# One strip of a fused convolution loads all its window rows instead of taking its middle row by direct matmuls

## What is computed

```python
# 1: mix the 4x4 patches of 8x8 pixels and the channels, and add the input
out = einsum('oi,nikj->nokj', g_weight, patches(x)) + x          # -> cen
# 2: for each shift 1 and 3 and four directions: product of the two differences
prod = (cen - shifted(cen, d)) * (cen - shifted(cen, -d))
att  = max over shifts of (min over directions) + mean over shifts of (min over directions)
# 3: depthwise 3x3 convolution, 1x1 convolution, gate
g = pointwise(depthwise3x3(att))
result = cen * sigmoid(g) + cen
```

## Time and profile before

| | us |
|---|---|
| Median of 3 runs | 104.37 |
| Lowest and highest run | 103.74, 104.5 |
| The profiled execution | 103.87 |
| Its span, first to last instruction | 102.1 |
| Busy TensorE / VectorE / ScalarE / GpSimd | 83.3 / 89.9 / 54.4 / 86.7 |

### The profile page before, as it was taken

One profiled execution on the slowest core, in us unless ns is written; L12 is line 12 of the kernel. 1 busy time (PEld: TensorE's weight loads), 2 busy tenths in 40 slices (PEclk: granted clock), 3 DMA queues, 4 the chain that ended last, 5 costly groups with the idle time before them and its releaser, 6 DMA issues.

```text
span 102.1 us, 2342 instructions
## 1 busy us (share of the span) xinstructions
PE 83.3 (82%) x924; PEld 43.2 (42%) x924; DVE 89.9 (88%) x129; ACT 54.4 (53%) x94; POOL 86.7 (85%) x79
## 2 busy tenths in 40 slices
PE   4997899999999659494998759997355988969970
PEld 2196788777787322222322212324021224413430
DVE  6044699999999999999999999999799999999970
ACT  3201455555576573945756995198674314708620
POOL 6400999999999999999999999999999999877600
PEclk9999999999999999999999999999999999999999
DMA  3999500000000079920039930203988535960085
GB/s 45 353 290 394 185 6 0 6 0 6 0 3 6 0 137 172 250 99 0 0 65 234 260 100 6 103 0 75 232 268 278 117 70 116 231 129 6 0 316 198
DMA packets 7306, 12.14 MB, mean 119 GB/s; under 512 B 800, under 2 KB 2816, under 8 KB 7296
## 3 DMA queue, kind: packets, MB, share of 16 engines
q1 hardware_dynamic: 6768, 10.93, 39.1%
q10 hardware_dynamic: 528, 1.07, 3.4%
HBM read 3.22 MB, written 2.10 MB: 52 GB/s over the span
## 4 chain that ended last, share of the span: by engine, by line
DVE 51%; PE 20%; POOL 11%; issue 6%; ACT 5%; DMA 4%; POOLq 0%; DVEq 0%; ACTq 0%
DVE slots L705 19%; DVE m L723 17%; PE slots L927 8%; POOL u L235 8%; DVE m L702 6%; PE slots L893 5%; DMA early<-in_first_dram 4%; PE acc L868 3%; ACT slots L599 2%; POOL m L527 2%; PE acc L812 2%; PE slots L812 2%; DVE u L235 1%; POOL early L399 1%; ACT early L625 1%
## 5 line engine op out<-in xcount | busy, mean ns | idle before, releaser
L235 POOL TENSOR_TENSOR u<-cen 128x1056 f32<-128x1056 f32 (+9 forms) x38 | 65.0, 1771 | 6.4 <-DVE u L235 6.4
L599 ACT ACTIVATE slots<-u 128x1024 f32<-128x1024 f32 (+2 forms) x43 | 32.0, 762 | 25.8 <-POOL u L235 16.9
L705 DVE TENSOR_TENSOR slots<-slots,u 128x1024 f32<-128x1024 f32 (+2 forms) x33 | 29.6, 895 | 0.9 <-ACT slots L599 0.9
L723 DVE TENSOR_TENSOR m<-slots,m 128x1024 f32<-128x1024 f32 (+1 forms) x27 | 25.7, 952 | 0.9
L822 PE MATMUL acc<-early 128*32 128x256 f32 (+1 forms) x512 | 24.8, 353 | 0.9 <-DVE cen L693 0.6
L822 PEld LDWEIGHTS acc<-early 128*32 128x32 f32 x512 | 19.9, 110 | 5.6 <-DVE cen L693 0.9
L927 PE MATMUL acc<-early,wc 128*32 128x512 f32 x120 | 13.7, 595 | 5.0 <-DMA early<-att 3.8
L868 PE MATMUL acc<-cen,eye 128*128 128x512 f32 (+1 forms) x16 | 8.5, 612 | 5.1 <-ACT cen L585 2.2
L927 PEld LDWEIGHTS acc<-early,wc 128*32 128x32 f32 x120 | 3.7, 109 | 14.5 <-issue 12.5
L585 ACT ACTIVATE cen<-acc 128x256 f32<-128x256 f32 (+1 forms) x18 | 5.5, 364 | 6.4 <-PE acc L812 5.6
L927 PE MATMUL slots<-early,wc 128*32 128x512 f32 (+1 forms) x96 | 7.9, 486 | 1.0 <-issue 1.0
(11 more groups left out here) (56 smaller groups left out, 76.3 us busy)
## 6 DMA issues: line engine op xcount, KB each, us to landing
early<-att SPq DMA_DIRECT2D x20, 204.0 KB, 3.7
early<-in_x_dram SPq DMA_DIRECT2D x4, 256.0 KB, 6.4
out_dram<-early SPq DMA_DIRECT2D x2, 512.0 KB, 3.7
early<-eye SPq DMA_DIRECT2D x1, 816.0 KB, 7.1
early<-in_g_weight_dram SPq DMA_DIRECT2D x3, 256.0 KB, 7.6
out_dram<-early SPq DMA_DIRECT2D x3, 256.0 KB, 2.1
early<-att SPq DMA_DIRECT2D x5, 136.0 KB, 4.9
early<-in_first_dram SPq DMA_DIRECT2D x2, 320.0 KB, 4.7
```

The source lines that it names most:

```text
L235: return eng.tensor_tensor(u[j][:, r0 - base:r1 - base, g], cen[:, PAD + r0:PAD + r1, g, left:left + wide], cen[:, PAD + r0 - dy:PAD + r1 ...
L599: nc.scalar.activation(slot_px(j, t), ahead(j, t), ACT.Copy).then_inc(u_copied, 1)
L705: nc.vector.tensor_tensor(slot_px(j, t), slot_px(j, t), here(j, t), ALU.mult).then_inc(multiplied, 1)
L723: nc.vector.tensor_tensor(dst, one, m[:, 0:n], ALU.max).then_inc(compared, 1)
```

## The change

Strip 5 is no longer direct: its four loads bring all three dy (96 partitions, 204 KB each instead of 136 KB), its zeroing DMA and its three direct matmuls are gone, and it uses the same weights as strips 0 to 4. Strip 6 stays direct, and its direct part and its zeroing keep their places (before strip 5, now written as `LAST - 2`). ScalarE issues quads 2 and 3 of strip 5, both after copy (5, 5), and none of strip 6; SyncE issues quads 0 and 1 of strip 5 and all of strip 6. ScalarE's moves of differences 3 and 4 stand behind copy (4, 4) instead of before it. The last copies are shared out anew: VectorE 3 + 3, all wide (before 4 + 5), ScalarE 3 + 4 (as many as before, but five wide ones instead of three), GpSimd 2 + 5, one of them wide (before 1 + 3, all narrow).

```diff
-    DIFFERENCES_AFTER = {(2, 6): [0], (3, 1): [1], (3, 6): [2], (4, 3): [3, 4]}
+    DIFFERENCES_AFTER = {(2, 6): [0], (3, 1): [1], (3, 6): [2], (4, 4): [3, 4]}
...
-    DIRECT = [5, 6]
+    DIRECT = [6]
     BLOCKS_BEFORE = (4, 2)
-    ACT_WINDOWS = {(5, 5): [(5, 3)], (5, 7): [(6, 0), (6, 1)]}
+    ACT_WINDOWS = {(5, 5): [(5, 2), (5, 3)]}
...
         DVE_PARTS, ACT_PARTS, POOL_PARTS = ({LAST: PARTS_OF[LAST][a:b], LAST + 1: PARTS_OF[LAST + 1][c:d]}
-                                            for a, b, c, d in ((0, 4, 0, 5), (4, 7, 5, 9), (7, 8, 9, 12)))
+                                            for a, b, c, d in ((0, 3, 0, 3), (3, 6, 3, 7), (6, 8, 7, 12)))
...
             for s in range(LAST):
-                if s == DIRECT[0]:
+                if s == LAST - 2:
                     for strip in DIRECT:
                         zero_rows(strip)
...
-                if s == DIRECT[0]:
+                if s == LAST - 2:
                     for strip in DIRECT:
                         convolve_direct(strip)
                 convolve(s)
```

## The result

The median of 22 runs of the changed kernel is 104.72 us (104.06 to 106.48), that of the kernel before in the same series 104.15 us (22 runs, 103.64 to 104.65). The ratio is 1.0048, 95% interval 1.0028 to 1.0068; it leaves out the three longest executions of the changed kernel (105.73, 106.42 and 106.48 us). So the change costs 0.2 to 0.5%, well inside one per cent.

What follows compares the result with a forecast made beforehand. Two close bounds, the last result and the DMA store queue; after the change the queue alone: +0.85 us later start, about -0.55 us closed hole, so +0.3 us and 104.7 us. Range 103.5 to 105.6 us.

Steps and rivals of the forecast that it cites:

- Step 1: Moves of differences 3 and 4 behind copy (4,4): VectorE's 0.57 us wait goes, 0.35 us gained, capped by ScalarE's bend.
- Step 2: ScalarE's two strip 5 loads after copy (5,5): issues at 84.0 and 84.64, copy (5,6) near 85.3, cost zero.
- Step 3: Without direct matmuls, TensorE starts strip 5 at 90.2 after its window, ends at 98.2 (bounds 97.9 and 100.0) instead of 98.90.
- Rival C: Strip 5's larger loads collide: window lands at 92.0, TensorE ends at 100.0, total 105.4 us; chance 0.06.
- Step 4: SyncE's changed load issues, 0.6 to 0.75 us each, are hidden in the gap before store 2: no cost.
- Step 5: GpSimd's seven last copies take 2.74 us, unit 2's result ends at 96.98, store 2 0.85 us later; VectorE's long copy shrinks.
- Rival B: Each of six GpSimd last copies waits for a 0.29 us VectorE copy: 1.75 us more, 106.4 us; chance 0.12.
- the long pair of the earlier trace: Near the end, VectorE's 2.29 us copy beside GpSimd's 2.23 us result of unit 2, excluding each other by shared ports.
- Step 6: Five final stores: DMA engines busy from 97.85, ending at 101.25 to 101.45 instead of 101.1; all stores waiting by 99.1.
- Rival A: Last computed result, not the store queue, sets the end: 0.7 to 1.0 us less, 103.5 us; chance 0.16.

Runs made afterwards that it cites:

- before_moves: Kernel before with only ScalarE's two moves of differences put behind copy (4,4): 103.94 us, ratio 0.9965.
- before_loads: Kernel before with only strip 5 not direct and the new load issue places, old split and old place of the moves: 105.34 us, ratio 1.0062.
- after_oldparts: Changed kernel with the old split of the last copies (VectorE 9, ScalarE 7, GpSimd 4): 103.88 us, ratio 0.9960 to the kernel before.
- after_vector: Changed kernel with unit 2's result on VectorE after its six copies instead of on GpSimd: 102.98 us, ratio 0.9896 to the kernel before.
- before_parts: Kernel before with only the new split of the last copies: 105.02 us, ratio 1.0055.
- second series: Changed kernel run again without edit, five rounds beside the kernel before: 104.71 us, 12 runs, ratio 1.0017.
- after_order: Changed kernel with SyncE storing unit 3 before unit 2: 104.07 us, ratio 0.9998 to the kernel before.
- loads_warm: Kernel before with strip 5 not direct, the new loads and two unread matmuls ahead of strip 5: 104.11 us, ratio 0.9987.
- after_warm: Changed kernel with two unread matmuls between strip 6's direct part and strip 5: 104.58 us, ratio 1.0043 to the kernel before.

## Why the prediction was right

It had 104.7 us, 0.3% above the median then shown, from +0.3 us on the span. Measured: 104.72, +0.48% and +0.17% in two series, +0.2 us of span. The mechanism (the store queue behind a later result of unit 2) came out, and so did the size on the span. That the microseconds agree to 0.02 is luck: the 104.37 it started from is the median of three runs, the kernel before had 104.15 in the series of the result, and the difference there is 0.57 us, with executions in it whose clock fell, which the sum didn't have.

*Step 1, the moves.* VectorE's wait of 0.57 us went. L745 of stage 4 started at 84.45, 0.42 us earlier (0.35 in the sum), and waited 0.17 us for the bend, as the step had it. L782 started 0.28 us earlier (91.42 for 91.70). Alone, the step is worth 0.35% (before_moves).

*Step 2, ScalarE's two issues.* They stand at 83.90 and 84.65 (84.0 and 84.64 in the text), the first of them ahead of the bend's end (84.42). Copy (5,6) starts at 85.59, 0.3 us later than written, and came only just in time: without the new place of the moves (before_loads), and with it in after_oldparts too, VectorE waited 0.16 us for it. The cost of zero holds for this execution and is no margin.

*Step 3, strip 5.* TensorE started it at 89.76 (90.2) and ended at 97.74 (98.2), inside its bounds. The row it took as the nearest was misread: there were no stores beside strip 3's loads (the next one is issued at 75.47, behind them), but strip 4's four loads in the same queue. What the step did not have is that such a wait, where it is over 2 us, can let the granted clock fall, at 1.7 us more for the last four strips. Rival C had a TensorE end of 100.0 but put it down to the window's landing. In 3 of 22 runs of the first series the time is above 105.7 us. All three have the same mean granted clock, 0.951, the lowest of the series; the one whose trace is shown has three stretches of low clock. So two things stand in the sum as nothing that are not always nothing, the clock here and the copy's wait in step 2. The first is the larger, and in the changed kernel it shows in part of the executions only.

*Step 4, SyncE.* Its six load issues end at 88.59 (83.85 + 4.74), 8.5 us ahead of store 2. No cost.

*Step 5, the copies.* GpSimd's seven: 2.67 us (2.74). Result over at 97.03 (96.98). Store 2: 97.05 (97.0). VectorE's long copy gone, as written. Rival B (6 x 0.29 us more) didn't come: while VectorE copied, GpSimd's copies were not slower than before. So what holds for the long pair of the earlier trace rows was not seen between these short copies.

*Step 6, the stores.* Full from 98.0 to 101.3 (97.85 to 101.25 or 101.45). The last store was issued at 99.42 and not ahead of 99.3: with stores waiting in the queue, three of the issues take 0.64 to 0.78 us instead of 0.34. It cost nothing.

*Rival A* was ruled out by the DMA rate, 374 GB/s where it needed 514. (The prediction said that no row shows more than 336; the kernel before itself has 388 from 97.0 to 98.3, which changes nothing.) By experiment the other order of things was then made: in after_vector, with store 2 gone early, the last store is issued at 98.89, right after the last result (98.44 to 98.86), and the span is 1.2 us shorter.

The parts do not add to the whole. Alone they give -0.35% (moves), +0.62% (loads) and +0.55% (split), together +0.82% against +0.17 to +0.48%. Part of it may be that the moves shorten TensorE's idle time ahead of strip 5 (2.21 us without them, 1.72 with), and so save the clock, and part that VectorE's wait for copy (5,6) is there in before_loads and not in the changed kernel; the intervals of +-0.3% for each part leave that open.

## What to carry to other kernels

The chain of waits ends at the last computed result. Where stores follow each other in one queue, look at when the first of them is issued and whether the DMA engines are full from there to the end: if they are, a faster engine behind the head of the queue gains nothing. A later head costs what the holes behind it don't take up: 0.2 of 0.9 us in the changed kernel, 0.7 of 1.3 us in before_parts. An earlier head gained most here (after_vector: 1.3 us earlier, 1.2 us less span). Before giving work to an engine because it has the fewest copies, see what is queued behind them there; and before removing matmuls that lie in a wait, see whether they fill the wait of a transfer anyway, and what keeps the clock up once they are gone. The version to use is either one with unit 2's result on VectorE, about 1.0 to 1.1% below the kernel before, with intervals from 0.7 to 1.5% (0.9896 with strip 5 by windows, 0.9888 direct); the two cannot be told apart.

## What had not been expected of the hardware

TensorE's granted clock fell to the lower of its two levels (1.2 GHz) after an idle time of 2.07 us (after_oldparts), 2.21 us (before_loads) and 2.78 us (changed kernel, first series), and stayed at 1.00 (2.4 GHz) after 1.72 us (second series) and 1.82 us (after_vector). But the length of the idle time alone doesn't decide it: in the kernel before TensorE waited 2.71 us ahead of strip 3 and the clock stayed at 1.00, while in the first series of the changed kernel it waited 2.68 us there and the mean clock of the next 3.3 us was 0.54 (timeline, then window):

```profile
76.05 6.93 PE L927 MATMUL acc<-early,wc 128*32 128x512 f32 x48 [2.68 <-DMA early<-att]
```

```profile
76.00:79.30 3.30, 3.25 (x20) 1.00 (x24) 3.23 (x4) 1.04 (x1) 3.30 (x3) 0.54 0.91 257
```

The same wait, 2.65 to 2.79 us ahead of strip 3, is in all thirteen profiled executions, and the clock fell in three of them (2.65 us in before_parts, 2.68 in the first series, 2.72 in after_order) and held in the others, after_oldparts with 2.65 among them. What tells them apart was not found. Nor is a low clock a property of the change: executions of the kernel before have mean clocks from 0.951 to 1.00 too. What the change added, by these traces, is one more place where it can fall, ahead of the last strips. 1.88 us of matmuls in the gap ahead of strip 5 took the tail of the times away in one kernel (loads_warm) and changed nothing that can be measured in the other (after_warm).
